# Rotated q and k groups kept in HBM by partition, and read back in rows of 8 KB with two transfers for q

## The reference

```python
q = (x @ Wq).reshape(B, T, H, 2 * DH)     # H = 16 heads, DH = 32
k = (x @ Wk).reshape(B, T, KV, 2 * DH)    # KV = 4; v likewise
q1, q2, k1, k2 = rope(each half of 32)
a1 = softmax(q1 @ k1.T / sqrt(DH) + mask); a2 = softmax(q2 @ k2.T / sqrt(DH) + mask)
out = (a1 - lam * a2) @ v                 # each kv head serves 4 q heads
x = layernorm(x + groupnorm(out) @ Wo)
```

## Time and profile before

| | |
|---|---|
| median of three runs | 2042.45 us (2035.61 to 2043.52) |
| profiled execution | 2053.17 us, its span 2051.3 us |
| mean granted TensorE clock | 0.925 of full speed |
| TensorE matmul, VectorE, ScalarE, POOL busy | 83%, 68%, 57%, 29% of the span |
| SP's DMA queue (q1) | 238.98 MB in 112272 packets, 41.6% of 16 engines |

### The profile page before, as it was taken

One profiled execution on the slowest core, in us unless ns is written; L12 is line 12 of the kernel. 1 busy time (PEld: TensorE's weight loads), 2 busy tenths in 40 slices (PEclk: granted clock), 3 DMA queues, 4 the chain that ended last, 5 costly groups with the idle time before them and its releaser, 6 DMA issues. The chain is left out here.

```text
span 2051.3 us, 36805 instructions
## 1 busy us (share of the span) xinstructions
PE 1706.9 (83%) x9698; PEld 1270.7 (62%) x9699; DVE 1389.8 (68%) x3225; ACT 1166.7 (57%) x3378; POOL 585.5 (29%) x480
## 2 busy tenths in 40 slices
PE   4578899899889889889889889783999999999600
PEld 3355666666656656656665666442999999999600
DVE  2589888888888988888888898734333333333385
ACT  2478788688777877777877877822222222222133
POOL 2232232432331331242242242011633342100173
PEclk8799999999999999999999999975999999999855
DMA  7975574574474474575466565113543344433285
GB/s 253 294 210 141 137 194 121 161 213 114 143 209 134 143 216 125 137 215 153 136 206 165 145 189 150 54 69 140 165 125 118 92 133 151 128 102 93 78 270 194
DMA packets 142469, 318.74 MB, mean 155 GB/s; under 512 B 16720, under 2 KB 19408, under 8 KB 140272
## 3 DMA queue, kind: packets, MB, share of 16 engines
q1 hardware_dynamic: 112272, 238.98, 41.6%
q0 software_dynamic: 15072, 50.74, 7.4%
q10 hardware_dynamic: 14976, 27.27, 3.5%
HBM read 215.21 MB, written 109.05 MB: 158 GB/s over the span
## 5 line engine op out<-in xcount | busy, mean ns | idle before, releaser
L806 ACT ACTIVATE expd<-S,neg_max 128x128 f32<-128x128 f32 (+3 forms) x1024 | 531.5, 536 | 161.2 <-DVE neg_max L961 159.0
L961 DVE TENSOR_REDUCE neg_max<-S 128x2 f32<-128x768 f32 (+3 forms) x384 | 399.9, 1041 | 164.9 <-PE S L650 155.9
L992 DVE SCALAR_TENSOR_TENSOR mixed<-expd,rho 128x384 f32<-128x384 f32 (+3 forms) x512 | 335.4, 675 | 0.0
L646 PE MATMUL S<-kT,qT 128*128 128x256 f32 (+2 forms) x1024 | 278.5, 374 | 20.7 <-ACT expd L806 11.2
L818 ACT ACTIVATE probsT<-PTp 128x512 f32<-128x512 f32 (+2 forms) x384 | 205.2, 534 | 114.7 <-PE PTp L661 112.8
L661 PE MATMUL PTp<-ident,mixed 128*128 128x128 f32 x1280 | 215.8, 284 | 53.5 <-DVE mixed L992 49.0
L1372 ACT ACTIVATE xT_hi<-xTp 128x512 fp32r<-128x512 f32 x72 | 43.1, 599 | 358.0 <-DVE yo L1553 352.4
L646 PEld LDWEIGHTS S<-kT,qT 128*128 128x128 f32 x1024 | 163.8, 194 | 123.2 <-issue 83.1
L700 PE MATMUL tail<-wo,ctxT 128*128 128x512 f32 x480 | 225.6, 594 | 0.5
L538 POOL TENSOR_TENSOR swapped<-swapped,rope_t 128x512 f32<-128x512 f32 x80 | 104.1, 1301 | 420.7 <-DVE swapped L954 420.7
L806 ACT ACTIVATION_READ_ACCUMULATOR expd<-S,neg_max 128x1 f32 x1024 | 217.2, 212 | 0.0
(11 more groups left out here) (224 smaller groups left out, 3675.1 us busy)
## 6 DMA issues: line engine op xcount, KB each, us to landing
qT<-parts_rows SPq DMA_DIRECT2D x256, 256.0 KB, 4.3
parts_rows<-parts SPq DMA_DIRECT2D x160, 256.0 KB, 2.3
wqk<-wqk_split SPq DMA_DIRECT2D x75, 512.0 KB, 6.1
xin<-expert_in_rows SPq DMA_DIRECT2D x72, 256.0 KB, 3.0
expert_out_rows<-yo ACTq DMA_DIRECT2D x72, 256.0 KB, 3.2
kT<-parts_rows SPq DMA_DIRECT2D x64, 256.0 KB, 4.5
x<-in_x SPq DMA_DIRECT2D x8, 1024.0 KB, 7.2
x_rows<-x SPq DMA_DIRECT2D x8, 1024.0 KB, 7.3
```

Source lines behind the costliest of these rows:

```text
L646: nc.tensor.matmul(S[s % 2][:, k * slot:k * slot + w], qT[kv % 2][:, 2 * h + c, i * P:(i + 1) * P], kT[kv][:, c, 0:w], start=(k % per_bank ...
L806: ex = nc.scalar.activation(expd[s % 3][:, k * slot:k * slot + w], S[s % 2][:, k * slot:k * slot + w], ACT.Exp, bias=neg_max[s % 3][:, k:k ...
L961: nc.vector.tensor_reduce(neg_max[s % 3][:, 0:k], v, AX, ALU.max, negate=True).then_inc(max_ready, 1)
L992: ins = nc.vector.scalar_tensor_tensor(out=mixed[sl % 3][:, a * 256:a * 256 + w], in0=e2, scalar=rr[:, i, h:h + 1], in1=e1, op0=ALU.mult, ...
```

## The change

`parts_dram` is laid out as 2 buffers x 2 parts x 32 x 4 x 512 in place of 2 x 2 x 128 x 512: the four rows that end in one partition lie side by side, 8 KB in all. A store now writes 2 KB pieces in the order "block, row in the block". A read takes rows of 8 KB. For k there are still four reads into 32 partitions each. For q there are two, one of each part, into 64 partitions; the source is the part's 32 rows, repeated twice. `parts_out` has a semaphore for each part, and a part's reads are issued when that part has landed. Since q's reads now count 32 and k's 64, the totals for `stacked` are summed over the groups.

```diff
-GROUP_COUNT = 64
+GROUP_COUNT = {"q": 32, "k": 64}
...
-    parts_dram = nc.dram_tensor("parts_rows", [2, 2, P, T], F32, kind="Internal").ap()
+    parts_dram = nc.dram_tensor("parts_rows", [2, 2, P // 4, 4, T], F32, kind="Internal").ap()
...
-        parts_out = [sem(f"parts_out{r}") for r in range(2)]
+        parts_out = [[sem(f"parts_out{r}_{side}") for side in range(2)] for r in range(2)]
...
+        ALL = [g for g in HEAD if g[0] != "v"] + [g for g in SEQ if g[0] != "v"]
+        PER_HALF = sum(GROUP_COUNT[kind] for kind, _ in ALL[LEAD - 2::2])
+        assert PER_HALF == sum(GROUP_COUNT[kind] for kind, _ in ALL[LEAD - 1::2])
+
+        def head_total(i):
+
+            return sum(GROUP_COUNT[kind] for kind, _ in ALL[i % 2:i + 1:2])
+
         def stack_total(b, idx):
 
-            return GROUP_COUNT * (NGRP // 2 * b + (LEAD - 2 + idx) // 2 + 1)
+            return PER_HALF * b + head_total(LEAD - 2 + idx) if idx >= 0 else PER_HALF * (b - 1) + head_total(LEAD - 2 + NGRP + idx)
+
+        def parts_total(n):
+
+            return 16 * (n // 2 + 1)
+
+        def stored_total(b, idx):
+
+            return 16 * (NGRP // 2 * b + (LEAD - 2 + idx) // 2 + 1)
...
-            def spread(kind, j, n, r2, total, free):
+            def spread(kind, j, n, r2, stored, free):
 
                 for side, done in ((0, hi_done), (1, lo_done)):
                     sp.wait_ge(done, n + 1)
                     apart(sp)
-                    sp.dma_start(parts_dram[r2, side], parts[r2][:, side, :].bitcast(F32)).then_inc(parts_out[r2], 16)
+                    sp.dma_start(parts_dram[r2, side].rearrange("p r t -> r p t"), parts[r2][:, side, :].bitcast(F32)).then_inc(parts_out[r2][side], 16)
                 at_least(sp, scores_ready, free)
                 apart(sp)
-                sp.wait_ge(parts_out[r2], total // 2)
-                apart(sp)
-                for k in range(4):
-                    here = slice(k * DH, (k + 1) * DH)
+                for side in range(2):
+                    sp.wait_ge(parts_out[r2][side], stored)
+                    apart(sp)
+                    rows = parts_dram[r2, side].rearrange("p r t -> p (r t)")
                     if kind == "q":
-                        side, dst = k // 2, qT[j // 2 % 2][here, 4 * (j % 2):4 * (j % 2) + 4, :]
-                    else:
-                        side, dst = k % 2, kT_all[here, 2 * j:2 * j + 2].rearrange("p a c t -> p (a c) t")
-                    sp.dma_start(dst.bitcast(F32), parts_dram[r2, side].rearrange("(r p) t -> p r t", p=DH)) \
-                      .then_inc(stacked[r2], 16)
+                        dst = qT[j // 2 % 2][2 * DH * side:2 * DH * (side + 1), 4 * (j % 2):4 * (j % 2) + 4, :]
+                        sp.dma_start(dst.rearrange("p r t -> p (r t)").bitcast(F32),
+                                     rows.unsqueeze(0).broadcast_to([2, DH, 4 * T])).then_inc(stacked[r2], 16)
+                        continue
+                    for k in (side, side + 2):
+                        dst = kT_all[k * DH:(k + 1) * DH, 2 * j:2 * j + 2].rearrange("p a c t -> p (a c t)")
+                        sp.dma_start(dst.bitcast(F32), rows).then_inc(stacked[r2], 16)
...
-                            high_part(group_no(b, idx), half(b, idx), stack_total(b, idx) - GROUP_COUNT)
+                            high_part(group_no(b, idx), half(b, idx), stack_total(b, idx) - GROUP_COUNT[SEQ[idx][0]])
```

More of the change, by code:

```diff
@@ L461, in _ @@
             for i, (kind, j) in enumerate(HEAD[:LEAD - 2]):
-                spread(kind, j, i, i % 2, GROUP_COUNT * (i // 2 + 1), 0)
+                spread(kind, j, i, i % 2, parts_total(i), 0)
             for g in SEQ[:7]:
@@ L497, in body @@
                     free = (b * KV + kv_of) * NU if kind == "q" else (b * KV + (0 if j == 1 else 2)) * NU
-                    spread(kind, j, group_no(b, idx), half(b, idx), stack_total(b, idx), free)
+                    spread(kind, j, group_no(b, idx), half(b, idx), stored_total(b, idx), free)
                     if idx == 1 and not first:
@@ L929, in _ @@
                 if 4 <= i < 7:
-                    high_part(i - 4, (i - 4) % 2, GROUP_COUNT * ((i - 4) // 2))
+                    high_part(i - 4, (i - 4) % 2, head_total(i - 4) - GROUP_COUNT[HEAD[i - 4][0]])
                 act.wait_ge(wraw_in[(0, 1, 1, 2)[i] if i < 4 else 3], 16 * ((1, 2, 2, 1)[i] if i < 4 else 7))
```

## The result

| | before | after |
|---|---|---|
| median | 2041.16 us (4 runs) | 3202.56 us (4 runs, 3189.91 to 3204.12) |
| ratio | | 1.5686 (95% interval 1.5641 to 1.5730) |
| profiled execution, span | 2053.17, 2051.3 us | 3202.28, 3200.4 us |
| mean granted clock | 0.925 | 0.776 |

The prediction said 4090 us, with a range from 2750 to 4600 and 0.86 on slower. The sign and the mechanism came out; the size of one term did not.

A forecast was written before the change was run, and what follows sets the result against it. Busy TensorE bounded the kernel, transfers hidden; afterwards q reads on two engines bound attention. Profiled 2053.2 + 2027 (eight batches) - 64 (last batch) + 81 (start) = 4097, said as 4090 us; range 2750 to 4600.

The forecast's parts named there:

- Issues worth nothing, cover of 4 to 24 us: SP's queue in attention: 128 fewer issues, 55 us of queue time, worth 0; reads hidden by about 4 to 24 us slack.
- the third case: Rival: q and store transfers still use all sixteen engines, 2040 us; chance 0.14 together with only the stores being confined.
- Shares of the outermost dimension: Attention's q reads and stores: dealt out by outermost dimension, so a q read gets 2 engines and a store 4.
- The rate of an engine: Attention's DMA: 13.3 GB/s per engine for q reads (25.1 the other end), 25.1 for stores (13.3 the high end).
- my ends of 39.4 and 20.9 us for a q group: Time of a q group's two reads on two engines: 39.4 us at 13.3 GB/s, 20.9 at 25.1.
- that case (between the first two): Rival: partial stagger of the two engines reading q, 2900 to 4090 us; chance 0.12, shared with reads alone confined.
- The stores: Attention's stores on four engines: 2.6 us each, 5.2 a pair at 25.1 GB/s.
- stores alone confined: Rival: only stores lose engines, a pair 4 us longer, within a few us of 2042; 0.14 together with sixteen engines.
- The phases: Attention's four phases per batch, summed in SP's queue order: 110, 108, 94 and 105 us, a batch of 417.
- head and last batch: Bare q groups and stores before the first batch add 81 us; the last batch, leaving out three groups, subtracts 64.
- Stalls in mid phase worth nothing: Within attention phases: ScalarE's high-part copy and weight loads queued behind q reads stall, but end earlier, costing 0.
- Clock and experts: Whole kernel: clock falls below 0.96, half-clock TensorE work still fits the phases; experts and combination change by 0.

The follow-up runs named there:

- all_wide: store_wide with q's repeat moved inside, each HBM row into two neighbouring partitions, k's rows interleaved to match, still two q reads; 2038.35 us, 0.9982 of the kernel before.
- store_wide: The changed kernel with weight columns permuted on the host so each store is one plain 128 x 512 block; q's two reads kept; 3075.05 us.
- pad2: Against store_wide: HBM rows in two padded blocks of 16, four q reads with 2 outermost, no repeat, shares into partitions 0-15 and 16-31; 2847.61 us.
- pad4: Like pad2 but four padded blocks of 8 rows, so q's four reads have 4 outermost; stores wide, in blocks of 32 partitions; 2402.82 us.
- reads4: The changed kernel with q read by four transfers of 32 rows into 32 partitions each; stores stay 4 outermost; 2083.9 us, 1.0219 of the kernel before.
- four_wide: store_wide with q read by four transfers of 32 rows into 32 partitions, so every transfer has 32 or more outermost; 2037.64 us, ratio 0.9988.
- two_copies: store_wide with each part stored twice in HBM, q's read taking its two shares from the two copies, still partitions p and p+32; 3014.57 us.

## Why the prediction was right, and where it missed

*Issues worth nothing, cover of 4 to 24 us.* Right. all_wide has the halved issues and gains 4 us, the start included. The estimate of 2040 for sixteen engines, the third case, is what all_wide measures.

*Shares of the outermost dimension.* Right, and shown three ways: shares of 0.13 with 2 outermost (the changed kernel, store_wide, pad2), 0.25 with 4 (pad4, and the stores of reads4), and the whole loss gone with 32 (four_wide, all_wide). The rule of the Trainium skill (DMA: Bandwidth & Descriptors, "Why a DMA increments its semaphore by 16 and not by 1"), the largest number up to 16 that divides the slowest dimension of both sides, agrees with every run, for 2, 4 and 32; no run here has another count. pad2 shows that it is the count and not the repeat.

*The rate of an engine.* This is the term that was mis-sized. I took 13.3 GB/s for q's reads throughout. Measured is a mixture: in some groups 29 to 37 GB/s for the pair, so 14.5 to 18.5 each, for up to 12 us on end (18 in store_wide), then 53, which is 26.5 each. Between my ends of 39.4 and 20.9 us for a q group, the batch of 307.3 us lies at 39.4 - (417 - 307.3)/8 = 25.7, if the whole miss is put on the reads; an estimate. In the row that I took the price from, sixteen engines crowd into one block of 32 partitions all the time. The reading that fits the runs is that two engines at p and p+32 are in each other's way only while they are in step, and that they come apart; no view shows the step itself. I had named that case (between the first two) and gave it too little weight. What parts them, and why some groups begin apart, is open; that neighbouring work on the queue gives one of them a lead is only argued. The port rule of the Trainium skill (SBUF — State Buffer, "Door 1: The DMA port swizzle") puts p and p+32 on one port. It agrees with pad2 and two_copies; but the pair moved 29 to 37 GB/s where one engine out of step moves 26.5, so together they got more through than one.

*The stores.* The engine work was right, what it meant was not. I wrote that stores alone confined would miss no phase beyond the tightest slack, within a few us of 2042: reads4 is 42 above. I had worked out the slack of 4 us and the cost of 4 us, took the one to cover the other, and left out that the low half's reads wait for the low half's store once more. Beside the slow reads, on the other hand, the stores cost less than their 3.9 us a group (127 us in all), as they hid a landing.

*The phases.* The order was right: phase 2, whose first group is stored ahead, is the shortest (67.3), phase 0 the longest (83.6), as in 94 and 110. But they are 67 to 84 us long where I had 94 to 110, and the engines' share in attention fell to 0.27, not to a fifth. The growth of the shown batch, 8 x (307.3 - 163.6) = 1150, meets the measured 1149 by luck, as it is one of the longer ones: over six batches the loads of x stand 302.7 us apart (473.00 to 2289.22), against 161.2 before (246.16 to 1213.35). That makes 8 x 141.5 = 1132, and 17 are left for head and last batch, which nearly cancel, as they did in the sum (81 - 64).

*Stalls in mid phase worth nothing.* Half right. They are 433 us of the waits (299.1 and 134.4). The sum leaves them out, so what they delay must be made up by a shorter wait for q at the phase's end; that was not tested by itself. A reader who went by the waits on q at the phases' starts alone would find 683 us and miss the rest.

*Clock and experts.* Right: the mean clock fell to 0.776, and the experts' stage still runs at 0.94.

## What to carry to other kernels

Before writing a transfer as one access pattern, look at the count of its outermost dimension on both sides: with 2 or 4 there it ran on 2 or 4 of the 16 engines. Put a repeat inside, not in front, or keep the several wide transfers; permuting columns on the host can make a store plain. Larger rows are worth nothing where the destination's partitions set the rate: read the GB/s of the stretch in which the engines are full before paying for them.

## What the runs showed of the hardware that I had not expected

- Two engines that fill partitions p and p+32 move 29 to 37 GB/s together in some stretches and 53 in others, with the same bytes; on 0 to 15 and 16 to 31 (pad2) 338 of 361 windows are at 47 or more.
- An issue can itself be held. Behind two q reads and a weight load, the two stores took 13.99 and 12.26 us to issue (13.2 and 11.5 of it in the second instruction alone), where it was 1.68 before. With the wide stores in the same place it is 1.53 (store_wide, 805.46), but there a weight load behind two q reads and an x load took 11.29 (732.23). That the queue takes only so much work for an engine, and SP stands still beyond that, is the reading; the limit was not measured.
- Reads into 16 partitions, with all 16 engines busy, moved 123 to 127 GB/s (pad2's reads of k, 128 KB each), against 213 for 32 partitions and 401 for 128:

```profile
812.00:814.00 2.00, 2.00 (x12) 1.66 (x11) 1.63 (x4) 2.00 (x12) 0.00 (x0) 1.00 1.04 127
814.00:816.00 2.00, 2.00 (x15) 1.63 (x13) 1.78 (x4) 2.00 (x11) 0.00 (x0) 1.00 1.01 123
```
